# A third relu of the channel mixing on ScalarE, and new orders of work for all engines, in a fused two-stage kernel

## What is computed

```python
def time_mix(x, ...):                      # a linear recurrence over time
    xk, xv, xr = (x * tm + time_shift(x) * (1.0 - tm) for tm in (tmk, tmv, tmr))
    return sigmoid(xr @ Wr) * wkv(w_decay, u_first, xk @ Wk, xv @ Wv) @ Wo
def channel_mix(x, ...):                   # H = 512
    xk, xr = (x * tm + time_shift(x) * (1.0 - tm) for tm in (f_tmk, f_tmr))
    k = square(relu(xk @ fWk))             # (tokens, 512): four blocks of 128
    return sigmoid(xr @ fWr) * (k @ fWv)
def attn(x):
    x = x + lif(time_mix(layer_norm(x)))   # lif: spikes of a leaky neuron
    return x + lif(channel_mix(layer_norm(x)))
def ffn(x):
    h = silu(x @ w1.T * w1_s) * (x @ w2.T * w2_s)
    h = gelu(h @ h1.T * h1_s); h = gelu(h @ h2.T * h2_s)
    return h @ w3.T * w3_s
x = x + layernorm(attn(layernorm(x)))
x = x + layernorm(ffn(layernorm(x)))
```

## Time and profile before

| | us |
|---|---|
| median of 3 runs | 657.61 (657.49 to 659.11) |
| the profiled execution | 658.89 |
| its span, first to last instruction | 656.9 |
| PE busy | 586.7 (89%) |
| DVE busy | 556.3 (85%) |
| ACT busy | 535.3 (81%) |
| POOL busy | 418.5 (64%) |

### The profile page before, as it was taken

The page is one execution under the profiler, slowest core; times in us unless marked ns, Lnnn a source line. Parts: engine busy times, 40 slices in busy tenths (PEclk is TensorE's granted clock), DMA queues, the critical chain, the costliest instruction groups (busy, mean ns, idle before and its releaser), DMA issues. The chain is left out here.

```text
span 656.9 us, 9756 instructions
## 1 busy us (share of the span) xinstructions
PE 586.7 (89%) x2241; PEld 362.5 (55%) x2241; DVE 556.3 (85%) x1538; ACT 535.3 (81%) x849; POOL 418.5 (64%) x571
## 2 busy tenths in 40 slices
PE   1366599999999999999999999999999999999994
PEld 0122247575656666565756566665746666656662
DVE  2978699989999999989999999999999899875543
ACT  4767397979799897979797998979797988958673
POOL 3553346768676777767777767776858665563442
PEclk9659699999999999999999999999999999999998
DMA  8010001001010101010010101010000101000001
GB/s 292 0 33 16 18 1 33 1 18 32 18 32 17 33 17 32 17 33 1 17 33 17 32 18 32 17 33 17 5 29 0 33 0 33 1 16 2 16 1 32
DMA packets 26574, 17.02 MB, mean 26 GB/s; under 512 B 1168, under 2 KB 25744, under 8 KB 26256
## 3 DMA queue, kind: packets, MB, share of 16 engines
q1 hardware_dynamic: 26512, 16.34, 8.2%
HBM read 12.14 MB, written 4.19 MB: 25 GB/s over the span
## 5 line engine op out<-in xcount | busy, mean ns | idle before, releaser
L906 ACT ACTIVATE hid<-p_f,scale 128x512 f32<-128x512 f32 x128 | 87.9, 686 | 65.0 <-PE p_f L2255 64.5
L2255 PE MATMUL p_f<-a_lo,w_hi 128*128 128x512 f32 x320 | 134.1, 419 | 1.6 <-DVE a_lo L289 0.7
L2255 PE MATMUL p_f<-a_hi,w_hi 128*128 128x512 f32 x320 | 125.9, 393 | 0.0
L2255 PE MATMUL p_f<-b_lo,w_hi 128*128 128x512 f32 x256 | 111.4, 435 | 2.3 <-DVE b_lo L289 0.9
L2255 PE MATMUL p_f<-b_hi,w_hi 128*128 128x512 f32 x256 | 100.7, 393 | 0.0
L900 ACT ACTIVATE a_hi<-hid 128x512 fp32r<-128x512 f32 x128 | 79.1, 627 | 2.9 <-DVE hid L1640 1.6
L432 POOL TENSOR_TENSOR nd<-factors,pq 128x512 f32<-128x512 f32 x32 | 38.7, 1209 | 62.9 <-DVE pq L1507 62.9
L289 DVE TENSOR_TENSOR a_lo<-hid,a_hi 128x512 fp32r<-128x512 f32 x96 | 65.7, 704 | 9.4 <-ACT a_hi L900 8.9
L2255 PEld LDWEIGHTS p_f<-a_lo,w_hi 128*128 128x128 f32 x320 | 60.3, 189 | 21.1 <-issue 7.0
L416 POOL TENSOR_TENSOR rstd<-var,minus_half 128x4 f32<-128x4 f32 x64 | 70.0, 1098 | 2.2
L289 POOL TENSOR_TENSOR b_lo<-hid,b_hi 128x512 fp32r<-128x512 f32 x32 | 45.4, 1432 | 38.6 <-DVE fired_all L1548 26.2
(11 more groups left out here) (143 smaller groups left out, 1437.8 us busy)
## 6 DMA issues: line engine op xcount, KB each, us to landing
xa<-in_x SPq DMA_DIRECT2D x16, 256.0 KB, 2.8
xb<-in_x SPq DMA_DIRECT2D x16, 256.0 KB, 3.0
out<-y_out SPq DMA_DIRECT2D x15, 256.0 KB, 3.3
kk<-in_ffn SPq DMA_DIRECT2D x1, 1024.0 KB, 6.5
hid<-in_ffn SPq DMA_DIRECT2D x1, 1024.0 KB, 8.9
mix<-in_mix SPq DMA_DIRECT2D x1, 512.0 KB, 6.5
gate<-in_ffn SPq DMA_DIRECT2D x1, 512.0 KB, 5.1
mix<-in_mix SPq DMA_DIRECT2D x1, 320.0 KB, 3.8
```

The lines of the kernel that those rows point to most:

```text
L906: act.activation(hid[:, m], p_f[m % 2][:, :], ACT.Gelu, scale=scale[:, 1 + layer, m:m + 1]).then_inc(s_gelu[layer], 1)
L2255: last = pe.matmul(out_, w[:, b], x[:, k], start=(k == 0 and t == 0), stop=(k == n - 1 and t == len(terms) - 1))
```

## The change

ScalarE now makes relu(g, 2) too, so VectorE makes relu(g, 0) alone. No other instruction is added, removed or given to another engine. All orders (opening, turn and ending of POOL, ACT, DVE and PE) are written anew. The point at which a turn begins has moved too, so a turn's list starts at another step; what matters is the cyclic order. The diff, cut to two of the lists:

```diff
@@ VectorE, turn(g)
+                low(3, g[4], 2)
+                bounds(g[1])
+                relu(g[2], 0)
...
-                f0(g[3])
-                relu(g[2], 2)
@@ ScalarE, turn(g)
-                tanh_2(g[2])
-                exp_table()
-                exps(g[1], 0)
-                exps(g[1], 1)
-                square(g[2], 0)
-                relu(g[2], 1)
-                f0(g[3])
+                relu(g[2], 2)
+                f0(g[3])
+                square(g[2], 0)
                 square(g[2], 1)
                 output_scaled(g[4])
+                square(g[2], 2)
                 relu(g[2], 3)
-                square(g[2], 2)
...
+                tanh_2(g[1])
+                exp_table()
+                exps(g[0], 0)
+                exps(g[0], 1)
+                relu(g[1], 1)
```

More of the change, by code:

```diff
@@ L733, in ending @@
                 offset_5(G[13])
+                low(2, G[14], 0)
+                neurons(1, G[15])
                 norm_5(G[13])
[L735 to L738, removed]
                 low(2, G[14], 2)
@@ L1155, in ending @@
                 gelu(1, G[10], 1)
+                neuron_input_1(G[12])
+                gelu(1, G[10], 2)
                 high(2, G[10], 1)
-                gelu(1, G[10], 2)
                 high(2, G[10], 2)
@@ L1218, in ending @@
                 high(3, G[11], 1)
+                bounds(G[14])
                 gelu(2, G[11], 2)
@@ L1959, in ending @@
                 low(3, G[10], 3)
-                relu(G[12], 2)
-                terms(G[13], 0)
                 sum_over_time(G[13], 1)
@@ L1996, in ending @@
                 low(2, G[11], 3)
+                norm_2(G[13])
                 excess(G[14])
-                norm_2(G[13])
+                bounds(G[14])
                 residual_3(G[12])
@@ L2003, in ending @@
                 mix_2(G[13], 1)
+                norm_4(G[12])
+                low(3, G[11], 3)
+                low(3, G[11], 1)
+                relu(G[13], 0)
                 low(3, G[11], 2)
-                norm_4(G[12])
-                low(3, G[11], 1)
-                bounds(G[14])
-                relu(G[13], 0)
-                low(3, G[11], 3)
                 sum_over_time(G[14], 1)
                 f0(G[12])
-                relu(G[13], 2)
+                terms(G[14], 0)
                 denominator(G[14])
@@ L2325, in opening @@
                     channel_v(G[0], 0)
-                    after(pe, s_z2, G[0].n)
-                    turn_1(G[2])
                     channel_v(G[0], 1)
@@ L2359, in onset @@
                     channel_k(G[1], 1)
+                    after(pe, s_bv[0], G[1].n)
+                    v_product(G[2])
                     after(pe, s_relu[0], G[1].n)
@@ L2500, in onset @@
                     channel_k(G[3], 0)
+                    after(pe, s_gate, G[1].n, HB, 4)
+                    v_product(G[4])
                     after(pe, s_tanh_r2, G[3].n)
@@ L2578, in turn @@
                     channel_k(g[1], 0)
+                    after(pe, s_gate, g[3].n, HB, 4)
+                    v_product(g[0])
                     after(pe, s_tanh_r2, g[1].n)
@@ new lines, in turn @@
+                    channel_k(g[1], 3)
+                    after(pe, s_relu[2], g[1].n)
+                    channel_v(g[1], 0)
+                    after(pe, s_f0_hi, g[2].n)
+                    after(pe, s_f0_lo, g[2].n)
+                    turn_5(g[3])
+                    channel_v(g[1], 1)
+                    after(pe, s_f_cm, g[3].n)
+                    to_gate(g[2], 0)
+                    after(pe, s_gelu[2], g[3].n, HB, 4)
+                    to_value(g[2], 0)
+                def ending():
@@ L2710, in ending @@
                     spikes_turned(0, G[13])
+                    after(pe, s_gelu[1], G[11].n, HB, 2)
+                    hidden(1, G[11], 3)
                     after(pe, s_fired[0], G[13].n)
@@ L2812, in ending @@
                     channel_k(G[14], 2)
+                    after(pe, s_gate, G[12].n, HB, 4)
+                    v_product(G[15])
                     after(pe, s_z2, G[14].n)
@@ L2818, in ending @@
                     channel_k(G[14], 3)
-                    after(pe, s_relu[2], G[14].n)
-                    channel_v(G[14], 0)
+                    after(pe, s_f_cm, G[12].n)
+                    to_gate(G[13], 0)
                     after(pe, s_f0_hi, G[13].n)
@@ L2882, in ending @@
                     last_product(G[13])
-                    after(pe, s_relu[1], G[15].n)
-                    channel_k(G[15], 3)
+                    after(pe, s_relu[2], G[15].n)
+                    channel_v(G[15], 0)
+                    after(pe, s_f_cm, G[13].n)
+                    to_gate(G[14], 0)
                     after(pe, s_f0_hi, G[14].n)
```

842 lines of the change are left out of this document (410 added, 432 removed).

## The result

| | before | now |
|---|---|---|
| median (5 runs each) | 659.10 us (657.49 to 659.22) | 662.19 us (661.10 to 663.93) |
| ratio | | 1.0069, 95% interval 1.0047 to 1.0092 |
| span of the profiled execution | 656.9 us | 662.1 us |

The changed kernel is slower. The forecast was no change, 657.6, with a range up to 661.8; the time lies just above the range. (The median of before was 657.6 in the three runs that the forecast started from and is 659.1 in these five.)

A forecast was written before the change was run, and what follows sets the result against it. The prediction took a 36.15 us loop of 20.65 ACT, 1.78 norm_1 with hand-over and 13.72 PE as the bound. Opening -5.2 + 0.5, turns +4.7, ending 0.0 sum to 0.0: 657.6 us, range 652.8 to 661.8.

The forecast's parts named there:

- The turn of 0.48 - 0.09 + 0.20: Steady turn: relu on ACT, less what the order returns, plus residual_5's new place; 0.59 longer, +4.7 us in 8 turns.
- rival B: Turns: POOL's residual_5 starts before DVE's low(2, g, 1), making DVE's low part 1.15 late; 665.2 us, chance 0.07.
- The signs that I had named: Gelu every 36.6 to 36.9, ACT stretch 21.0, PE waiting about 1 before turn_1; wrong if turn 36.2 or turn_2 after 73.
- The relu's term: Steady turn: the relu moved to ACT lengthens its stretch without idle time by 0.48 us a turn.
- The order gives 0.12 back: ACT in the turn: silus no longer held up by late PE return 0.09 us, between 0 and 0.15.
- DVE's relief is worth nothing: Steady turn: taking the relu off DVE (0.685 us there) gains nothing by itself, as DVE is not in the loop.
- residual_5's term: POOL in the turn: residual_5 ahead of low(2, g, 2) makes that low part late; +0.20 a turn, 0 to 0.40.
- The opening's term: Opening: spikes and k_product ahead of the branch, statistics reordered, DVE's relu gone; -5.2 us, then +0.5 for the relu.
- the branch: PE in the opening: its 4.10 us hole moves to where PE has nothing to do; 3.8 us gained.
- The 1.2 of the rstd order: POOL in the opening: statistics of G[1] pass ahead of G[0]'s residual, so norm_2 of G[1] gains another 1.2 us.
- The ending: Last groups: a wait for gates goes, about -1.0, and the relu on ACT adds about +1.0; sum 0, known to 2 us.
- rival C: Opening gives little, as the hole outlasts turn_2's readiness or PE's clock stays low; gain 1.8, 661.0 us, chance 0.13.

The follow-up runs named there:

- r5: The changed kernel with DVE's low(1, g, 0) ahead of swiglu(g, 2) in its turn, nothing else; ratio 1.0003 against the kernel before, 656.4 us.
- r4: The kernel before with relu(g, 2) of the 8 turns moved from VectorE to ScalarE behind relu(g, 1); ratio 1.0073, 661.5 us.
- r3: As r1, with relu(g, 2) of the 8 turns back on VectorE ahead of low(3, g, 3); ratio 1.0068, turn 37.05 us.
- r7: As r5, with relu(g, 2) of the 8 turns back on VectorE behind low(3, g, 3); ratio 1.0031, turn 36.91 us.
- r6: As r5, with residual_5 behind low(2, g, 2) on POOL again; ratio 0.9988, turn 36.54 us.
- h2: The kernel before with the spikes of G[1] and k_product of G[2] ahead of PE's branch, nothing else; ratio 0.9950, 653.25 us.
- h1: The changed kernel's opening up to the second hidden layer of G[0], then turns and ending of the kernel before; ratio 0.9976.
- h4: The kernel before with PE's branch turned round, so that the short program that runs stands first; ratio 0.9938.
- h6: The kernel before with the branch's long program replaced by a single wait, the short one still in the Else; ratio 0.9956.
- h3: The changed kernel with k_product(G[2]) and the spikes of G[1] behind PE's branch again; ratio 1.0159, 666.7 us.
- r1: The changed kernel with one extra 128x4 product of constants on POOL ahead of low(1, g, 1) in its turn; ratio 1.0048, 659.6 us.

## Why the prediction was wrong

**The failed step is that the sum has no term for a race at low(1, g, 0).** The turn of 0.48 - 0.09 + 0.20 puts it at nothing, and rival B (0.07) put it at another place. I had the mechanism, with its sizes, from the earlier trace rows, and looked for it where POOL's own order changes (residual_5 against low(2, g, 1)). It came at low(1, g, 0) against low(1, g, 1), where DVE's order changes: low(1, g, 0) went behind ratio_end and swiglu(g, 2), which on DVE take 0.60 and 0.66 from start to start. In the trace of before it starts 0.86 ahead of POOL's; moved back by 1.26 it would start 0.40 behind, in the middle of POOL's step, and with both engines' neighbours shifted it starts 0.03 behind. The sum would have warned of a meeting, though not of a tie. It could have been made for every pair of two-input steps on DVE and POOL that the change moves, and I made it for one. The race, 4.6 us in the profile and 4.3 by the ratios, turns a kernel that equals the one before (r5, 1.0003) into one 0.7% slower. At the place that I named, nothing was stretched on DVE in any turn.

The signs that I had named don't catch this. ACT's stretch is 20.98 as written, PE waits for n ahead of turn_1 (0.69, where I had about 1) and no longer for bv, turn_2 of G[1] comes before 73, and no turn is 36.2 or less. Only the length of the turns, 36.5 or 37.4 where I had 36.6 to 36.9, pointed at something else.

The Trainium skill (SBUF — State Buffer, Who interferes with whom) says that a DVE instruction with two SBUF inputs contends with a GpSimd instruction that reads SBUF, that the shared ports are an exclusive lock, and, of DVE's two-port modes, that the other engine is blocked fully. The rows here agree for two inputs too: 1.51 and 1.79 are what was left of POOL's step and 0.55.

**The relu's term** held: 0.48 forecast, 0.45 measured by itself (r4). The order gives 0.12 back, where I had 0.09. What I had wrong is that DVE's relief is worth nothing: in the order of before it is (r4), but in the new one DVE has no room for the relu (r3, r7).

**residual_5's term** was 0.20 and is 0 (r6). I had compared POOL's times with when PE took low 2 before, without asking when ACT's high part for it comes. The steady turn without the race is thus 36.53, 0.39 longer (0.32 on ACT, 0.07 in PE's part), 3.1 us in 8 turns in place of 4.7.

**The opening's term** was over-sized: with the relu's 0.5 it was -4.7, and the experiments give -1.6. Of its parts the branch was right: 3.8 forecast, 3.4 measured in h2 from spikes to turn_2, 3.3 in time (2.2 to 4.4). The 1.2 of the rstd order were wrong: add_1 to norm_2 of G[1] went from 3.95 (69.60 to 73.55) to 3.58 (66.53 to 70.11), since DVE's scan stands between them in both. And the rest of the new opening costs 1.7 (h1 against h2), of which I had forecast 0.5, for the relu.

In the two profiled executions the opening also differs by what TensorE's clock did. Up to the spikes of G[0] h2 and before run the same list, and reach them at 61.34 and at 64.29; over 40 to 60 the granted clock was 0.95 in the one and 0.74 in the other. So the -2.4 of the first table mixes the change with chance: from turn_2 of G[1] to the gelu of G[0] the changed kernel took 36.31 in its profile, with a clock of 0.52 over 70 to 80, and r5, with the same opening, 34.33, with 0.89. Of the seven kernels with this opening as it stands, the six others reached the gelu of G[0] at 103.8 to 105.3 in their profiles and the changed kernel at 107.7; the two with the old one, before and r4, at 110.0 and 107.3. That is why the differences above are taken from ratios of several runs. The windows of h2 and of before over 40 to 60:

```profile
40.00:60.00 20.00, 13.19 (x33) 4.40 (x31) 16.88 (x37) 17.42 (x28) 8.49 (x13) 0.95 0.05 14
```

```profile
40.00:60.00 20.00, 15.38 (x31) 5.41 (x29) 14.78 (x32) 16.24 (x28) 7.26 (x11) 0.74 0.04 14
```

**The ending** was 0 with 2 us of doubt and came out at -0.8 in the profile.

**The account:** branch -3.3, rest of the opening +1.7, 8 turns +3.1, 5 lost races +4.6 (4.3 by the ratios), ending -0.8: +5.3, against 4.5 measured (3.1 to 6.1). The first two are known to 1.1 and 1.5 us only. The errors of the forecast pull against each other: the race that it lacked and the opening that it over-sized made it too low, by 4.6 and 3.1, and the turns and the ending made it too high, by 1.6 and 0.8. That it missed its range by only 0.4 us is luck. So is rival C's number, 661.0, the nearest to the measured 662.2: it has no race in it. C was right that the opening brings little, but for another reason than it gave: the branch brought what it should, and the moves beside it took half of that back.

The Trainium skill (Advanced Engine Details and Errata, Control Flow Timing) gives a compare-and-branch about 0.108 us. The far jump of before took 4.10. h4 and h6 can't test the figure, since a cost under the 0.89 and 1.01 for which PE waits there would be hidden.

**A faster version:** h2_branch_later, which keeps all of the kernel before and moves two steps of PE ahead of the branch, is 0.5% faster than before and 1.2% faster than the changed kernel. h4_branch_swapped, which only turns the branch round, gives as much (0.9938, 0.9914 to 0.9961).

## What to carry to other kernels

When orders are rewritten, list every pair of steps on VectorE and GpSimd that read two SBUF tiles and work out how far apart their starts come to lie, for the engine that moved and for the one that didn't. Here a pair that ended up level cost DVE what was left of POOL's step, in some repetitions and not in others. Windows of one repetition each find it at once: the same instructions, two lengths, and one engine busier in the long one. A step on a full engine costs its distance from start to start, and moving it off pays only if the engine that takes it has room there, which the busy share doesn't tell.

## What the runs showed of the hardware

- A jump on PE over a long program of instructions left PE idle for 4.1 us (4.10 in before and 4.12 in h3, shown as "issue"); over one instruction (h6), or with the arm that runs put first (h4), no hole was left beside waits of 0.89 and 1.01 for POOL.
- Low parts of 128x512 that started 0.03 us apart on DVE (0.68 when not held up) and POOL (1.27): the loser ended 0.55 after the winner when it was DVE and 1.12 after when it was POOL. DVE lost in 5 of the 8 turns of the changed kernel and in 7 of 8 in h3. POOL's start was the first in all 16, by 0.023 to 0.035, and between 0.029 and 0.031 both outcomes occur.
- With a step of 0.15 us more on POOL (r1) every turn took 36.67, against 36.53 in r5 and 36.51 in the changed kernel's short turns, though PE shows no wait for it.
